# Stage one of a four-layer block: values four batches behind the product, their weights fetched and split later and in two parts, tables made in later turns

## What is computed

```python
w = weight[adapter_ids]                      # (8, 512, 512)
x = x + jnp.einsum('bsi,boi->bso', x, w)     # "product"
# attention: 32 query heads, 8 key and value heads of 128
q = lora_linear(x, wq, aq, bq, adapter_indices)
k = lora_linear(x, wk, ak, bk, adapter_indices)
v = lora_linear(x, wv, av, bv, adapter_indices)
# lora_linear: x @ w + (x @ a[i]) @ b[i]
q, k = apply_rope(q), apply_rope(k)          # cos and sin of position * frequency
```

## Time and profile before

| what | value |
|---|---|
| median of 3 runs | 814.28 us |
| lowest and highest | 813.04 and 816.55 us |
| the profiled execution's own time | 815.11 us |
| its span | 813.2 us |
| busy PE, DVE, ACT, POOL over the span | 751.0, 535.0, 322.8, 302.8 us |
| stage one (to the barrier's end) | 116.4 us of the span |
| PE busy from 20 to 108 us | 68.74 us of 88.00 |

### The profile page before, as it was taken

How to read it: one execution, slowest core, us unless ns; L and a number is a source line. 1 busy time by engine, 2 the same in 40 slices (tenths; PEclk the granted TensorE clock), 3 DMA queues, 4 the chain that set the end, 5 groups by cost and what they waited for, 6 DMA issues and landing times. The chain is left out here.

```text
span 813.2 us, 13401 instructions
## 1 busy us (share of the span) xinstructions
PE 751.0 (92%) x4132; PEld 625.9 (77%) x4132; DVE 535.0 (66%) x1400; ACT 322.8 (40%) x924; POOL 302.8 (37%) x250
## 2 busy tenths in 40 slices
PE   3588979999789999999999999999999999987798
PEld 2476858787678888888888888888888888875686
DVE  3686634788576667676676667667676766754883
ACT  3535423211253454354435435345434533442540
POOL 3333223345372273255237236326424622510410
PEclk9899979999899999999999999999999999999799
DMA  8565267775123034024122304302502111600402
GB/s 275 196 219 190 66 172 220 217 235 185 34 66 117 1 112 136 1 64 142 39 64 69 111 2 127 116 0 65 165 15 64 65 39 37 138 10 24 111 27 78
DMA packets 61482, 81.59 MB, mean 100 GB/s; under 512 B 21174, under 2 KB 38742, under 8 KB 57862
## 3 DMA queue, kind: packets, MB, share of 16 engines
q1 hardware_dynamic: 60530, 79.83, 31.9%
q0 software_dynamic: 768, 1.25, 0.6%
q10 hardware_dynamic: 148, 0.07, 0.0%
HBM read 66.16 MB, written 15.48 MB: 100 GB/s over the span
## 5 line engine op out<-in xcount | busy, mean ns | idle before, releaser
L978 POOL TENSOR_TENSOR prob<-prob,rinv 128x512 f32<-128x512 f32 x64 | 66.7, 1043 | 210.2 <-DVE rinv L1064 210.2
L927 ACT ACTIVATE prob<-sm,nmax 128x128 f32<-128x128 f32 x256 | 99.8, 391 | 77.9 <-DVE nmax L1047 77.9
L971 POOL TENSOR_TENSOR qt<-qc,qs 128x512 f32<-128x512 f32 x60 | 78.1, 1301 | 97.1 <-DVE qs L1007 97.1
L1137 PE MATMUL ps_out<-wt_hi,v_hi 128*128 128x512 f32 x256 | 105.7, 413 | 4.4 <-DVE v_lo L1024 2.4
L916 ACT ACTIVATE v_hi<-ps_o 128x512 fp32r<-128x512 f32 x64 | 38.1, 595 | 162.0 <-PE ps_o L1125 162.0
L77 PE MATMUL ps_q<-x1t_hi,blk_hi 128*128 128x512 f32 x240 | 100.4, 418 | 0.0
L1139 PE MATMUL ps_out<-wt_hi,v_lo 128*128 128x512 f32 x256 | 100.3, 392 | 0.0
L1138 PE MATMUL ps_out<-wt_lo,v_hi 128*128 128x512 f32 x256 | 100.2, 391 | 0.0
L79 PE MATMUL ps_q<-x1t_hi,blk_lo 128*128 128x512 f32 x240 | 95.7, 399 | 0.0
L78 PE MATMUL ps_q<-x1t_lo,blk_hi 128*128 128x512 f32 x240 | 95.6, 398 | 0.0
L1007 DVE TENSOR_TENSOR qs<-ps_q,sin_t 64x512 f32<-64x512 f32 x120 | 82.7, 689 | 3.7
(11 more groups left out here) (212 smaller groups left out, 1732.3 us busy)
## 6 DMA issues: line engine op xcount, KB each, us to landing
wo_raw<-in_L_cond_wo_l SPq DMA_DIRECT2D x8, 1024.0 KB, 5.0
raw_w<-in_L_cond_wq_l SPq DMA_DIRECT2D x8, 1024.0 KB, 5.3
raw_b<-in_L_cond_bq SPq DMA_DIRECT2D x64, 128.0 KB, 3.6
w_raw<-in_L_cond_weight_t SPq DMA_DIRECT2D x7, 1024.0 KB, 5.8
v_hi_d<-v_hi SPq DMA_DIRECT2D x16, 256.0 KB, 2.5
v_lo_d<-v_lo SPq DMA_DIRECT2D x16, 256.0 KB, 3.1
k_rot<-kr SPq DMA_DIRECT2D x16, 256.0 KB, 2.8
kt<-k_rot SPq DMA_DIRECT2D x16, 256.0 KB, 2.7
```

The costliest lines, as they stand in the source:

```text
L927: e = act.activation(prob[i][:, h, :], sm[:, h, :], ACT.Exp, bias=nmax[i][:, h:h + 1], scale=-1.0, accum_out=rsum[i][:, h:h + 1])
L971: pool.tensor_tensor(qt[:, half, h, :], qc[:, :], qs[:, :], ALU.add).then_inc(q_done, 1)
L978: pool.tensor_tensor(prob[i][:, :, :], prob[i][:, :, :], rinv[i][:, :].unsqueeze(2).broadcast_to([P, G, T]), ALU.mult).then_inc(prob_done, 1)
L1137: pe.matmul(ps_out[:, :], ot_hi[:, q], wo_hi[:, h, :], start=(h == 0), stop=False)
```

## The change

Nothing is computed otherwise; instructions and transfers of stage one change places.

- `LAG = 4`: values(b-4) instead of values(b-2), so the loops of PE, ACT and DVE run to turn 11 instead of 9.
- SP: x[1] is issued ahead of w0_raw of batch 1; raw_w of block 0 moves from turn 1 to turn 2, behind w0_raw of batch 2; raw_b of block 0 moves to turn 3, behind w0_raw of batch 3; the adapters' picks and first loads come before x[2] and x[3]; block 1 is fetched in turn 6; stores start in turn 6.
- `block_part` is cut in two. Block 0: weights in turn 2, adapters' packs in turn 3. Block 1: weights in turn 8 and packs in turn 9, both behind that turn's values step. POOL's share of block 0 comes behind its share of batch 3.
- Tables: one quarter of `angles` a turn in turns 4 to 7, the Sin activations in turn 9, the mask in turn 10.

```diff
+        LAG = 4
...
+                        if b == 0:
+                            sp.dma_start(res[:, 1, :], x[1]).then_inc(x_in[1], 16)
                         if b == 1:
-                            for n in (1, 2, 3):
-                                sp.dma_start(res[:, n, :], x[n]).then_inc(x_in[n], 16)
-                            load_block_w(sp, 0)
                             sp.wait_ge(ids_in, 32)
                             picks.extend(sp.value_load(id_rows[0:1, 1, n:n + 1], min_val=0, max_val=bq4.shape[0] - 1) for n in range(B))
                             load_a(0)
                             load_a(1)
-                            load_block_b(sp, 0, picks)
+                            for n in (2, 3):
+                                sp.dma_start(res[:, n, :], x[n]).then_inc(x_in[n], 16)
                         if b == 2:
+                            load_block_w(sp, 0)
                             for n in range(4, B):
                                 sp.dma_start(res[:, n, :], x[n]).then_inc(x_in[n], 16)
                         if b >= 2:
                             load_a(b)
-                        if b == 5:
+                        if b == 3:
+                            load_block_b(sp, 0, picks)
+                        if b == 6:
                             sp.wait_ge(raw_lo_done, KC // 2 + PAIRS)
                             sp.wait_ge(raw_lo_pool, KC // 2)
                             load_block_w(sp, 1)
                             load_block_b(sp, 1, picks)
-                        if b >= 4:
-                            sp.wait_ge(v_lo_done, b - 3)
-                            store_v(sp, b - 4)
-                    for n in range(B - 4, B):
+                        if b >= LAG + 2:
+                            sp.wait_ge(v_lo_done, b - LAG - 1)
+                            store_v(sp, b - LAG - 2)
+                    for n in range(B - LAG - 2, B):
                         sp.wait_ge(v_lo_done, n + 1)
                         store_v(sp, n)
...
-                        if b == 1:
+                        if b == 3:
                             block_lo(1, 0)
                             block_lo(3, 0)
...
-                    for b in range(B + 2):
+                    for b in range(B + LAG):
                         if b + 1 < B:
                             turn_x(b + 1)
                         if b < B:
                             product(b)
-                        if b >= 2:
+                        if 2 <= b < B + 2:
                             turn_ax(b - 2)
                         if 1 <= b <= B:
                             adapters(b - 1)
-                        if b >= 2:
-                            values(b - 2)
+                        if b >= LAG:
+                            values(b - LAG)
...
-                    def block_part(n):
+                    def block_w_part(n):
                         act.wait_ge(raw_w_in, 16 * (n + 1))
                         if n == 1:
                             act.wait_ge(y_ready, B - 1)
                         for k in range(KC):
                             act.activation(blk_hi[n][:, k, :], raw_w[:, k, :], ACT.Copy).then_inc(raw_hi_done, 1)
+
+                    def block_b_part(n):
                         act.wait_ge(raw_b_in, 16 * B * (n + 1))
                         for p in range(PAIRS):
                             act.activation(blk_b[n][:, p, :], raw_b[:, p, :], ACT.Copy).then_inc(raw_hi_done, 1)
...
-                        if b >= 2:
+                        if 2 <= b < B + 2:
                             copy_axt(b - 2)
+                        if b >= LAG:
+                            values(b - LAG)
                         if b == B:
-                            block_part(1)
-                        if b >= 2:
-                            values(b - 2)
+                            block_w_part(1)
+                        if b == B + 1:
+                            block_b_part(1)
                         if b < B:
                             split_x1(b)
                         if b + 1 < B:
                             split_a(b + 1)
-                        if b == 1:
-                            block_part(0)
-                        if b == 4:
+                        if b == 2:
+                            block_w_part(0)
+                        if b == 3:
+                            block_b_part(0)
+                        if b == B + 1:
                             act.wait_ge(tab, 8)
                             act.activation(sin_t[:, :], ang[:, :], ACT.Sin).then_inc(sines, 1)
                             act.activation(cos_t[:, :], turns[:, :], ACT.Sin, bias=rope_cols[:, 3:4], scale=-1.0).then_inc(sines, 1)
...
-                        if b == B:
-                            block_part(1)
                         if 1 <= b <= B:
                             pack_ax(b - 1)
-                        if b >= 2:
-                            values(b - 2)
+                        if b >= LAG:
+                            values(b - LAG)
+                        if b == B:
+                            block_w_part(1)
+                        if b == B + 1:
+                            block_b_part(1)
                         if b < B:
                             split_x1(b)
                         if b + 1 < B:
                             split_a(b + 1)
-                        if b == 1:
-                            block_part(0)
-                        if b in (2, 3):
-                            angles(2 * (b - 2))
-                            angles(2 * (b - 2) + 1)
-                        if b == 5:
+                        if b == 2:
+                            block_w_part(0)
+                        if b == 3:
+                            block_b_part(0)
+                        if 4 <= b < 8:
+                            angles(b - 4)
+                        if b == B + 2:
                             mask_table()
```

More of the change, by code:

```diff
@@ L302, in _ @@
                     pool.dma_start(mask_u8[:, :], mask.rearrange("b t -> (b t)").partition_broadcast(P)).then_inc(tables_in, 16)
-                    for b in range(B + 2):
+                    for b in range(B + 1):
                         if b < B:
```

## The result

The changed kernel takes 805.1 us (median of 4 runs, 803.7 to 807.0), the kernel before 815.4 on the same chip. The ratio is 0.9878, with a 95% interval from 0.9844 to 0.9913: faster by 7 to 13 us. The forecast was 803.5, a gain of 10.8. The profiled execution took 803.7 us, its span is 801.7 against 813.2.

The account below looks back on a forecast made before the run. It took PE in stage one to be held up by other engines' lists and late weights, not PE work. Gains of 14.2 us less 3.4 for the clock left 10.8: 815.11 to 804.3, median 803.5, range 798.5 to 809.0.

Parts of the forecast that it names:

- x[1]: nothing.: Start of stage one: issuing x[1] ahead of the second weights gains nothing, since product(0) still waits for POOL.
- Third weights at 23.5, turn_x1(1) at 27.0.: Turn 1: third weights, issued ahead of raw_w and raw_b, land at 23.5, not 27.41; turn_x1(1) comes 3.5 us earlier.
- The fourth weights are late next, turn_x1(2) at 33.7.: Turn 2: 4.3 MB at 373 GB/s put the fourth weights at 30.7; turn_x1(2) comes 14.0 us earlier.
- Turn 3, 7.5 us.: Turn 3: ACT's copies and DVE's last subtraction and add set 7.5 us, so turn_x1(3) comes at 41.2.
- Turn 4, values(0) waits 0.6 us for raw_b's copies.: Turn 4: DVE's raw_b copies take 3.76 us, ending 0.6 after PE is ready; turn_x1(4) at 50.4.
- rival 4: No gain: DVE slowed beside POOL costs 10 us over block 0 and five turns, leaving 0.8, 813.5 us; chance 0.06.
- Turns 5 to 7: Turns 5 to 7 take 8.33, 8.33 and 7.93 us, PE's undisturbed pace, so turn_x1(7) comes at 75.0.
- The tail, 18.8 us from turn_x1(7) to v_lo(6).: End of stage one: values(4) to (6) run through one bank; v_lo(6) at 93.8, PE resumes 8.45 us later.
- The clock takes 1.5 at values(4) and 1.9 at product(4).: Stage one: low clock at values(4) and product(4) takes back 3.4 us, cutting the gain from 14.2 to 10.8.
- signs of being wrong: Fourth weights after 33, a turn from 5 to 7 over 9 us, repeated 5.5 us ps_y groups, or stage two changed.
- rivals 3 and 4: Rival 3: fourth weights land at 34, turn 2 grows 3.7 us, 807.2, chance 0.11; rival 4: DVE against POOL, 0.06.
- allowance of 0.8 us: Whole kernel: the median of the runs lies 0.8 us below the profiled execution, turning 804.3 into 803.5.

Follow-up runs that it names:

- e6: The changed kernel with x[1] issued behind the second weights again, as before the change: 809.1 us, one run.
- e8: The changed kernel with the tables put back (angles in turns 2 and 3, Sin in turn 4, mask in turn 5): ratio 0.9992 to the kernel before.
- e3: The changed kernel with x[1] to x[3], raw_w and raw_b of block 0 back ahead of the third weights: ratio 0.9922 to the kernel before.
- e2: The kernel before with only the tables moved: angles in turns 4 to 7, Sin and mask in turn 9 behind the last values step: ratio 0.9951.
- e12: The changed kernel with fourth and fifth weights fetched earlier, Sin in turn 8, a second values bank, block 2's raw_b issued in stage two: 797.8 us, ratio 0.9774.
- e5: The changed kernel with the two Sin activations in turn 8 instead of turn 9: 803.8 us, ratio 0.9883 to the kernel before.

## Why the prediction was right, and where its terms were off

Point by point, by its own steps:

- **x[1]: nothing.** Right, by e6.
- **Third weights at 23.5, turn_x1(1) at 27.0.** Right: 26.7. ACT split them at 22.80 without having waited.
- **POOL's wait of product(2) gone.** Right: the row of 4.7 us in the earlier trace rows has no successor in the new list.
- **The fourth weights are late next, turn_x1(2) at 33.7.** The mechanism is right: PE idles 3.40 us there, the longest gap left. The size is off by 1.9. They landed at 31.87 instead of 30.7 (the sum as written, 17.4 + 11.5 + 2, makes 30.9), and landing to turn took 3.7 us instead of 3.0, since DVE's second subtraction took 1.34 beside POOL. The engines were as full as forecast, but in the four stretches of 4 us from 20 to 36 they moved 417, 407, 305 and 298 GB/s, not 373 throughout.
- **Turn 3, 7.5 us.** It took 9.1. The chain over ACT is the forecast one, without a wait on it from 36.72 to 42.20. What I missed lies at both ends: turn_x1(2) ran at the low clock (1.12 us instead of 0.66), and DVE's subtractions beside POOL put turn_x1(3) 2.45 us behind ACT's last split instead of 1.3. Product(3), though slow, cost nothing here: PE was through its list at 43.43 and stood 1.22 us for DVE's add.
- **Turn 4, values(0) waits 0.6 us for raw_b's copies.** Wrong as a wait, right in sum (9.4 against 9.2). The copies took 2.73 us, not 3.76, and values(0) waited for nothing. The row of 3.76 us (102.88 to 106.64) was not one with POOL at rest, as I had read it: POOL worked until 104.10. DVE's subtractions of the sixth weights took 3.32 us instead of 1.3 and set the turn.

The POOL row of the kernel before, then the DVE rows of turns 3 and 4 in the changed kernel, and POOL's of the same time:

```profile
101.13 2.97 POOL L296 TENSOR_TENSOR wt_lo<-raw_w,wt_hi 128x512 fp32r<-128x512 f32 x2 [12.08 <-ACT wt_hi L450]
...
41.13 2.86 DVE L502 TENSOR_TENSOR wt_lo<-w_raw,wt_hi 128x512 fp32r<-128x512 f32 x2
...
46.85 2.73 DVE L161 SCALAR_TENSOR_TENSOR blk_b<-blk_b,rope_cols,raw_b 128x512 fp32r<-128x512 f32 x4
...
50.10 3.32 DVE L502 TENSOR_TENSOR wt_lo<-w_raw,wt_hi 128x512 fp32r<-128x512 f32 x2
...
38.68 3.08 POOL L301 TENSOR_TENSOR blk_lo<-raw_w,blk_hi 128x512 fp32r<-128x512 f32 x2 [2.65 <-ACT blk_hi L455]
...
41.73 3.39 POOL L312 TENSOR_TENSOR wt_lo<-w_raw,wt_hi 128x512 fp32r<-128x512 f32 x2
...
49.87 3.00 POOL L312 TENSOR_TENSOR wt_lo<-w_raw,wt_hi 128x512 fp32r<-128x512 f32 x2 [4.75 <-ACT wt_hi L421]
```

This is the mechanism of rival 4 at another place. Four copies with nobody beside them take 0.68 us each. Two subtractions beside POOL take 2.86 and 3.32 us, against 1.66 in turns 5 and 6, where POOL is nearly done when they start. The Trainium skill (GPSIMD Engine Reference, Specifications) names the shared SBUF interface. The trace agrees, and the prediction should have priced the subtractions by it, not only the copies. It weighed the row of 4.51 us only as a rival.

- **Turns 5 to 7, 24.6 us.** 25.0.
- **The tail, 18.8 us from turn_x1(7) to v_lo(6).** 18.8, and the gap ahead of values(7) 2.67. The 8.45 us of SP are 8.47.
- **The clock takes 1.5 at values(4) and 1.9 at product(4).** Wrong in both places. Values(4) took 3.26 and product(4) 2.99; product(3) was slow, 4.65, and so were the two turns ahead of it. The windows of tile ps_y show product(3) and product(4), with the granted clock behind the busy times of PE, PEld and DVE, 0.62 and 1.00, as in the earlier trace rows:

```profile
37.10:41.90 4.80, 4.66 (x12) 3.43 (x12) 0.00 (x0) 0.62 0.74 257
45.40:48.60 3.20, 3.00 (x12) 2.18 (x12) 0.00 (x0) 1.00 0.68 241
```

The prediction had 102.2 without the clock and 105.6 with its 3.4 us; stage two started at 106.4. Of the missing 4.2 us, 1.9 stood at turn_x1(2), 1.6 came in turn 3, 0.2 in turn 4 and 0.4 in turns 5 to 7 (the last 0.1 is rounding). So the sum was right to 0.8 us, but a good part of that is luck: an allowance made for the clock stood in for transfers and for DVE beside POOL.

None of its signs of being wrong came. The fourth weights landed before 33, turns 5 to 7 took 8.4, 8.7 and 7.9 us (9 was the bound), no product from turn 2 on took over 4.65 (5.5), and from stage two to the attention stage it is 96.1 us against 97.0 before. Parts of rivals 3 and 4 did: the late landing, 1.2 us of its 3.3, and DVE beside POOL.

The allowance of 0.8 us between the profiled execution and the median was the wrong way round: the profiled execution of the changed kernel, 803.7, was its fastest.

## What to carry to other kernels

Ask of each part of a reordering what it is worth alone and what it is worth with the others: here the lag alone lost 4 us of stage one, the tables alone won 3, and together with the moved transfers they won 10. Without the tables nothing was left of it (e8), without the moved transfers 4 (e3). That the lag is what frees the transfers is read from the lists: before, values(0) needs block 0 in turn 2. No run has the moved transfers and tables without the lag. Look at what ends a stage before putting work at its end, as e2 did. Follow the next transfer in the queue, and the one behind it: three orders of the same bytes moved the gap from turn 1 to turn 2 to turn 3. And price an engine's instruction by who works beside it at its new place, not by its mean.

## What the runs showed of the hardware

Two instructions of DVE with one tensor input from SBUF (L543 and L544) took 1.77 and 1.64 us beside a busy POOL, and 0.74 and 0.69 us where POOL stood still for the first and began only 0.5 us before the end of the second. The transfers don't explain it: the busy share of the DMA engines was 1.05 or more at the short ones and 0.00 at the 1.64 (e8, 45.4 to 47.0). Subtractions with two SBUF inputs took 0.69 alone and up to 5.24 us beside POOL. That one began at 14.84 and ended at 20.08, while POOL's four ran from 14.56 to 19.51:

```profile
13.80 0.69 DVE L502 TENSOR_TENSOR wt_lo<-w_raw,wt_hi 128x512 fp32r<-128x512 f32 x1 [0.66 <-ACT wt_hi L421]
...
14.84 5.24 DVE L502 TENSOR_TENSOR wt_lo<-w_raw,wt_hi 128x512 fp32r<-128x512 f32 x1 [0.34 <-ACT wt_hi L421]
```

The same kernel, executed twice, put the low clock at product(1) once and not the other time (4.40 and 3.03 us). The stretch from the start of stage two to the attention stage, the same instructions in all kernels but e12, took 94.7 us in e5 and 100.5 in e6. PE's wait for DVE's blk_b in it was 1.8 and 5.1 us, which is 3.3 of the 5.8; the cause of either was not looked for.
